# V products in every step of the biased thin attention, and the causal output copy behind the exponentials

## The reference

```python
att = jnp.einsum('bhqd,bhkd->bhqk', q, k) * (1.0 / math.sqrt(HS))
att = att + compute_bias(rel_emb, t, t)      # second one only; the first has a causal mask
att = jax.nn.softmax(att, axis=-1)
o = jnp.einsum('bhqk,bhkd->bhqd', att, v)
```

## Time and profile before

| | us |
|---|---|
| median of three runs | 7254.03 |
| the profiled execution | 7254.47 (span 7252.7) |
| 330 to 890 us, steady part of Aatt | 560 of it, some 30 batches: PE busy 490.44, DVE 357.96, ACT 336.70 |
| 2860 to 3700 us, steady part of Catt | 840 of it, some 30 batches: PE busy 727.65, DVE 787.95, ACT 549.56 |

### The profile page before, as it was taken

One profiled execution on the slowest core, in us unless ns is written; L12 is line 12 of the kernel. 1 busy time (PEld: TensorE's weight loads), 2 busy tenths in 40 slices (PEclk: granted clock), 3 DMA queues, 4 the chain that ended last, 5 costly groups with the idle time before them and its releaser, 6 DMA issues. The chain is left out here.

```text
span 7252.7 us, 109988 instructions
## 1 busy us (share of the span) xinstructions
PE 5933.6 (82%) x31088; PEld 3327.1 (46%) x31088; DVE 4632.3 (64%) x11759; ACT 2682.3 (37%) x6018; POOL 1326.4 (18%) x1059
## 2 busy tenths in 40 slices
PE   5788859979988887888863679977995888998979
PEld 2333334755456542333322443344553456554755
DVE  4666557734764557999968549973336765447736
ACT  0155614722364212666640115531110354224711
POOL 1211106110431012000000005530002431015100
PEclk9799979989999987999985789998998999999989
DMA  4333244662456434332322221123222456224641
GB/s 140 93 74 73 65 135 145 205 196 77 133 178 206 141 101 113 89 89 78 89 72 75 90 76 36 37 81 107 63 64 84 135 173 210 81 92 150 196 154 57
DMA packets 914603, 807.21 MB, mean 111 GB/s; under 512 B 241768, under 2 KB 770112, under 8 KB 913856
## 3 DMA queue, kind: packets, MB, share of 16 engines
q1 hardware_dynamic: 502064, 507.31, 24.1%
q10 hardware_dynamic: 389888, 274.83, 12.2%
q0 software_dynamic: 22144, 18.99, 0.8%
HBM read 506.25 MB, written 316.67 MB: 113 GB/s over the span
## 5 line engine op out<-in xcount | busy, mean ns | idle before, releaser
L1428 ACT ACTIVATE Catt_E<-Catt_t 128x512 f32<-128x512 f32 x1024 | 565.2, 595 | 308.3 <-DVE Catt_t L1391 259.1
L1377 DVE CUSTOM_DVE_ANT_0 Catt_S<-Catt_s,Catt_win 128x1024 f32<-128x1024 f32 x512 | 621.3, 1215 | 13.9 <-DMA Catt_win<-skewed 12.3
L1377 DVE CUSTOM_DVE_ANT_0 Aatt_S<-Aatt_s,Aatt_win 128x128 f32<-128x128 f32 (+7 forms) x512 | 373.5, 757 | 210.8 <-PE Aatt_s L1298 206.2
L1428 ACT ACTIVATE Aatt_E<-Aatt_t 128x512 f32<-128x512 f32 (+3 forms) x768 | 334.2, 493 | 236.8 <-PE Aatt_t L1330 188.4
L1327 PE MATMUL Catt_t<-Catt_Q,Catt_K 123*128 123x512 bf16 x1024 | 329.0, 383 | 100.2 <-ACT Catt_E L1428 69.2
L1298 PE MATMUL Catt_s<-Catt_K,Catt_Q 96*128 96x512 bf16 x1024 | 321.2, 396 | 51.0 <-DVE Catt_nmax L1377 30.0
L1391 DVE TENSOR_TENSOR Catt_t<-Catt_t,Catt_near 128x256 f32<-128x256 f32 (+2 forms) x640 | 281.3, 456 | 73.6 <-PE Catt_t L1327 66.1
L2399 PE MATMUL scan_cum<-scan_X,scan_upto 128*128 128x512 f32 x512 | 265.6, 609 | 26.4 <-DVE scan_X L2468 24.7
L1327 PE MATMUL Aatt_t<-Aatt_Q,Aatt_K 99*128 99x512 bf16 (+3 forms) x768 | 235.5, 333 | 56.6 <-ACT Aatt_E L1428 41.0
L1349 PE MATMUL Catt_o<-Catt_E,Catt_V 128*32 128x256 f32 x4096 | 273.9, 385 | 0.0
L2397 PE MATMUL scan_cum<-scan_X,scan_after 128*128 128x512 f32 x448 | 239.6, 617 | 39.8 <-DVE scan_pi L2479 39.8
(11 more groups left out here) (728 smaller groups left out, 14084.3 us busy)
## 6 DMA issues: line engine op xcount, KB each, us to landing
moe_cb<-c_s SPq DMA_DIRECT2D x16, 1024.0 KB
skewed<-lines POOLq DMA_DIRECT2D x8, 1920.0 KB
Catt_win<-skewed SPq DMA_DIRECT2D x16, 960.0 KB, 4.7
rec<-state_in_r ACTq DMA_DIRECT2D x32, 416.0 KB
scan_r<-rec SPq DMA_DIRECT2D x64, 208.0 KB, 2.5
Catt_near<-near_s SPq DMA_DIRECT2D x32, 384.0 KB
Aatt_Rb<-r_s ACTq DMA_DIRECT2D x32, 256.0 KB
v_s<-B0qkv_vo ACTq DMA_DIRECT2D x32, 256.0 KB, 2.1
```

Source lines behind the costliest of these rows:

```text
L1377: v.tensor_tensor_reduce(out=S[:, j % 2, 0:w], in0=s_ps[j % 2][:, 0:w], in1=win[:, 0 if causal else h, w0:w0 + w], scale=-1.0, scalar=BIG, ...
L1428: a.activation(E[:, kb % NB, h, lo:hi], bank(it, n)[:, 0:hi - lo], ACT.Exp, scale=scale).then_inc(exped, 1)
```

## The change

Catt calls `values` in every step instead of `values_of_block` in every second, at the same lag of 3. For Aatt the list of ACT has `exp` ahead of `move_out`, so that within the step that holds both, the copy and its DMA issue come behind the two exponentials; for Catt the list stays as it was. The number of banks is as before (three for `t`, one for `o`).

```diff
-            written_out(t, PAIRS, ST, ((0, scores), (TURN, turn_maxima), (LAG, scores_by_key), (LAG + 3, values_of_block)))
+            written_out(t, PAIRS, ST, ((0, scores), (TURN, turn_maxima), (LAG, scores_by_key), (LAG + 3, values_of_block if causal else values)))
...
-            written_out(a, PAIRS, ST, ((TURN, move_maxima), (LAG + 4, move_out), (LAG, exp), (LAG + 11, write_sums),
+            copy, exps = (LAG + 4, move_out), (LAG, exp)
+            written_out(a, PAIRS, ST, ((TURN, move_maxima), *((exps, copy) if causal else (copy, exps)), (LAG + 11, write_sums),
                                      (LAG + 15, spread_sums), (LAG + 23, store)))
```

## The result

The changed kernel takes 7194.16 us (7185.32 to 7197.32), the kernel before beside it 7251.62 us: a ratio of 0.992 with an interval of 0.9908 to 0.9933, or 57 us less. The forecast was 7219 us, with a range of 7203 to 7241. Measured again beside the last experiments it was 7187.42 us.

The account below looks back on a forecast made before the run. The prediction took DVE to bound Catt and PE's waits to count in Aatt. It subtracted 15.5 us (Aatt) and 19.7 us (Catt), 35.2 together, from 7254.5 for 7219 us, with a range of 7203 to 7241.

Parts of the forecast that it names:

- What bounds the kernel: Steady parts of both attentions: DVE leads Catt, busy 787.95 of 840 us; PE leads Aatt, 490.44 of 560.
- Part 1, the meeting: Catt, where two batches meet: shorter V group removes DVE's 0.61 us wait; 0.50 us a batch, 15.5 us in all.
- its own list: Signs of failure: DVE waits in steps that had none, a changed 1215 ns per mask, Catt's clock leaving 1.00.
- Part 2, behind the turn: Catt, behind the turn of the maxima: the 0.28 us wait goes, the 0.48 stays; 9.0 us in 32 batches.
- The split's cost: Catt: 0.10 us of PE per extra V group start, felt in four short DVE steps; 0.15 us a batch, 4.8 us.
- "slower" rival: Catt: a group of four costs more than half of eight, so PE becomes the bound; 7306 us, chance 0.05.
- The sum for Catt: Catt's terms together: 15.5 + 9.0 - 4.8 = 19.7 us, with bounds of 12 and 25.
- Part 3, Aatt: Aatt, copy behind exponentials: PE's 1.24 us wait goes, V starts 0.50 us earlier a batch; 15.5 us (11 to 18).
- The clock: Aatt loses at most about 6 us to clock dips, Catt none; counted as nothing, 0 to 6 us kept as upside.
- All waits gone: Rival: all DVE waits in Catt vanish (48 us), plus Aatt's 15.5 and 6 of clock; 7185 us, chance 0.10.
- Aatt nothing: Rival: in Aatt the later copy holds V until 539.86 after all; 7235 us, chance 0.08.
- Catt nothing: Rival: in Catt PE's new copy wait and group starts eat the gain, leaving Aatt's 15.5; 7239 us, chance 0.12.

Follow-up runs that it names:

- e7: Changed kernel with the V products of the first key block of each Catt batch again in one group of eight; 7209.37 us, ratio 0.9939.
- e6: Changed kernel with the copy behind the exponentials in Catt too, as in Aatt; 7262.62 us, ratio 1.0014 to the kernel before.
- e5: Changed kernel with ACT's order copy, two exponentials, DMA issue in both stages; 7193.36 us, ratio 0.9919 to the kernel before.
- e1: Kernel before with only Catt's V products in every step, Aatt unchanged; 7216.67 us, ratio 0.995.
- e4: Kernel before with Catt's undivided groups of eight V products moved one step later; 7257.04 us, ratio 1.0006.
- e2: Changed kernel with Catt's line taken back, so only Aatt's ACT order differs from the kernel before; 7229.21 us, ratio 0.997.
- e3: Changed kernel with all of Catt's V products one step later (lag 4); 7215.83 us, ratio 0.9943 to the kernel before.
- e8: Changed kernel with only key block 3's V products of Catt in fours, all others in eights; 7217.33 us, ratio 0.9958 to the kernel before.
- e10: Changed kernel with Catt's V products of units 0 to 10 one step later and, in both stages, the DMA issue behind the exponentials; 7174.13 us.
- e11: Kernel before with the sums' DMA issue moved behind the step's exponentials in both stages; 7206.37 us, ratio 0.9933.

## Why the prediction was wrong

The three places and what happens there were right. What failed are two terms of Catt's sum, both in the same direction: what a late product costs DVE was read from its idle time alone, and a cost was charged for the split that nothing paid.

**What bounds the kernel: right.** DVE in Catt, PE in Aatt. A mask still takes 1215 ns, the additions 564 for 563, and the clock in Catt is 1.00.

**Part 1, the meeting: mechanism right, size near.** 0.50 us forecast, 0.44 measured, and e7 ties them to the V group there. All predicted signs are there: V 0.06 behind the copy, 0.58 us of a new wait of PE, the addition of unit 4 late, the 0.61 gone. The chain from the copy's start to the addition of unit 5 is 3.74 us, where 3303.10 - 3299.43 = 3.67 were worked out; the 0.07 are the group of four, which takes 0.57 and not 0.50. The lateness of unit 4 was put at 0.15 us of waiting and is 0.36: the tile comes 0.07 later for the same reason, and DVE is there earlier, because the step ahead of it is 0.22 shorter (1.61 for 1.83). The forecast had not seen these 0.22. They don't add to the gain, since the chain through ACT sets the three steps (in e7 they are gone too, and the steps still take 5.74). By its own list the forecast was to be wrong if DVE waits appeared in steps that had none; that of unit 4 is one, and larger than it had allowed.

**Part 2, behind the turn: the step that failed.** The step was to take DVE's idle time ahead of an addition for all that a late product costs. 0.28 us were counted, from the bracket in the earlier trace rows; the three intervals with units 9, 10 and 11 went from 6.12 to 5.63 us, which is 0.49. The 0.48 stayed, as forecast. The rest has one source, which shows twice. The interval of unit 11 lost 0.36 (1.97 to 1.61). Behind each mask DVE reads the accumulator out; before, that was at

```profile
3314.68 0.08 DVE L1377 DVE_READ_ACCUMULATOR2_ANT Catt_nmax<- 128x1 f32 x1
```

and the addition came at 3315.03. In after both start at 3083.86. An addition that needs no waiting runs beside the read-out, so one with 0.28 in its bracket was really 3315.03 - 3314.68 = 0.35 late. Every bracket of these additions is 0.08 too small. And unit 9 lost 0.15 where no wait had been shown at all. The timeline of before, around unit 9:

```profile
3310.38 0.60 PE L1327 MATMUL Catt_t<-Catt_Q,Catt_K 123*128 123x512 bf16 x2
...
3310.53 0.25 DVE L1399 RECIPROCAL Catt_sums<-Catt_sums 128x16 f32<-128x16 f32 x1
...
3310.80 0.65 DVE L1391 TENSOR_TENSOR Catt_t<-Catt_t,Catt_near 128x128 f32<-128x128 f32 x2
```

and of after:

```profile
3079.27 0.60 PE L1327 MATMUL Catt_t<-Catt_Q,Catt_K 123*128 123x512 bf16 x2
...
3079.84 0.25 DVE L1399 RECIPROCAL Catt_sums<-Catt_sums 128x16 f32<-128x16 f32 x1
3080.01 0.60 DVE L1391 TENSOR_TENSOR Catt_t<-Catt_t,Catt_near 128x128 f32<-128x128 f32 x2
```

Before, the first of the two products ends at 3310.38 + 0.38 = 3310.76, and the addition starts at 3310.80, 0.27 behind the reciprocal's start; after, it ends at 3079.65, ahead of the reciprocal, and the addition starts 0.17 behind the reciprocal's start, within it. The two additions last 0.60 us for 0.65, which is the rest of the 0.15. The lateness was covered by a short instruction of DVE itself, so no idle time showed. The same stands ahead of unit 15, behind the read-out:

```profile
3292.80 0.60 PE L1327 MATMUL Catt_t<-Catt_Q,Catt_K 123*128 123x512 bf16 x2
...
3293.33 0.08 DVE L1377 DVE_READ_ACCUMULATOR2_ANT Catt_nmax<- 128x1 f32 x1
...
3293.43 0.43 DVE L1391 TENSOR_TENSOR Catt_t<-Catt_t,Catt_near 128x256 f32<-128x256 f32 x1
```

That interval fell from 1.59 to 1.47: another 0.12. This is why DVE's busy time fell with the same instructions. Counted from mask to mask over 30 batches, the mean is 26.29 us of busy time before and 25.91 after, 0.38 less, beside 0.72 less of idle time (1.69 and 0.97). The lengths of all its instructions added up are the same, 30.12 and 30.09 us a batch: they only overlap more.

**The split's cost: the second term that failed.** 0.15 us a batch were charged for the four short steps of DVE. Measured is nothing: the intervals of units 14, 15, 0 and 1 are 1.48, 1.47, 1.48 and 1.47. A PE step in the densest part of after is even longer than worked out:

```profile
3085.79 0.60 PE L1298 MATMUL Catt_s<-Catt_K,Catt_Q 96*128 96x512 bf16 x2
...
3087.33 0.60 PE L1298 MATMUL Catt_s<-Catt_K,Catt_Q 96*128 96x512 bf16 x2
```

1.54 us between the scores of two steps, where I had 1.48. Four such steps take 0.28 us of the lead that PE has from the steps before, and that lead holds: no interval there is longer than before by more than 0.01. The "slower" rival needed a fixed part of a group above 0.37; here a group of four lasts 3070.60 - 3070.03 = 0.57 us against 1.00 for eight, a fixed part of 0.14. The Trainium skill's rule ("TensorE: Matmul & The Clock Gate", packing small matmuls) would make each new boundary of a group exposed; the 0.10 to 0.14 us are there in PE's own time, and none of it reached the end, because PE was not what bound the stage. As a general rule the trace doesn't bear it out: in after the weights of a product of unit 4 (123 rows) load at 3070.83, while the scores' matmuls ahead of it (96 rows, 3070.60 to 3071.20) still run.

**The sum for Catt.** 0.63 forecast; 0.15 for the split not paid, 0.21 more around the turn, 0.12 at unit 15, 0.05 in units 7 and 8, 0.06 less at the meeting: 0.63 + 0.15 + 0.21 + 0.12 + 0.05 - 0.06 = 1.10, against 1.11 measured. Times 32 that is 15 us of the miss of 25; Aatt is 5 of it, and the rest lies outside both stages, within the spread of the executions.

**Part 3, Aatt.** 0.50 us forecast from bounds of 0.35 to 0.57, 0.61 to 0.62 measured, so just above the upper bound. The copy ended 1.72 us behind the mask matmul where 1.76 at the least had been worked out, for the case that it overlaps the exponentials; so that case is the right one, and the copy takes 0.60 us where 0.63 were put in. In 31 meetings it is 4 us. As forecast the 37.4 us are gone and 0.59 a batch took their place.

**The clock.** In Catt it stayed at 1.00 although PE now has short pauses everywhere, so the swing of the clock did not come. (The Trainium skill tells of it in "TensorE: Matmul & The Clock Gate", the section on a second failure mode; nothing in after shows it in Catt. It is near, though: with one long pause a batch, of 2.2 us, e6 shows the clock at 0.50 in 18 of 31 batches, and e5, whose PE pauses as in after, in one.) In Aatt the mean rose from 0.99 to 1.00: three stretches at 0.50 before, one now. A batch with one took 19.91 us before where the others took 18.37, so two fewer are about 3 us less, an estimate. That is the part of the 0 to 6 us held back as an upside that came. The count goes with the order of ACT in Aatt: the three kernels that wait 1.24 us there (before, e1, e4) have three, five and five such stretches, the eleven others none or one. In Aatt the medians of the batches are of batches without such a stretch.

**The rivals.** "All waits gone" (7185) is nearest in time but wrong as a mechanism: 28.8 us of DVE's waits are still there. "Aatt nothing" and "Catt nothing" fell with e1 and e2.

What stays open: why the interval of unit 8 is 0.07 to 0.21 us longer (1.81 in after, 1.91 in e3) in every kernel but e2 and e8, and why e6's clock fell behind some of its long pauses and not behind others.

## What to carry to other kernels

An idle time in brackets is a lower bound of what a late operand costs: a short instruction ahead of the wait can cover the lateness. Measure the interval from start to start of the engine that sets the pace, step by step, and forecast in intervals. Before a gate is removed, look for a second chain of the same length that ends at the same instruction; here taking away either of two gates gave 0.00 and 0.04 us a batch and both together 0.48. When a median of batches misses its forecast, look at the granted clock batch by batch; e6's median hid two kinds of batches. Where single steps of an engine that does not bind exceed the binding engine's step (PE's 0.44 + 0.44 + 0.10 + 1.00 = 1.98 us against 1.61), spreading them evenly is worth more than the fixed cost of more groups.

## What the runs showed of the hardware

- Four V matmuls take PE 0.57 us from the start of the group to the next instruction, eight take 1.00.
- A DMA issue on ACT between a copy and an exponential keeps them 0.73 us apart (3069.97 to 3070.70); without it they are 0.04 apart in e10 (3138.31 to 3138.35). Where the exponential's operand was itself 0.25 us late (e11), leaving the issue out gave 0.48. In e10 the issue, which comes behind both exponentials in the program, starts at 3138.50 while the first runs.
- DVE's addition starts within the run of its reciprocal (0.17 us behind the start of one that lasts 0.25) when its operand is early; busy time fell for that reason, with the summed lengths of its instructions the same (30.12 and 30.09 us a batch).
- A pause of 0.58 us in PE once a batch, and many short ones, left the granted clock of Catt at 1.00 in after (in e5, with the same pause, it fell to 0.50 once in 31 batches). A pause of 2.2 us once a batch (e6) was followed by 0.50 in 18 of 31 batches, at 1.48 us each.
